# Layer norms of a five-attention decoder: the normalising step moved from VectorE to ScalarE, with a shift made on GpSimd

## What is computed

```python
def _layernorm(x, axis=-1, eps=1e-05):
    m = jnp.mean(x, axis=axis, keepdims=True)
    v = jnp.var(x, axis=axis, keepdims=True)
    return (x - m) / jnp.sqrt(v + eps)
```

## Time and profile before

| | |
|---|---|
| median of 3 runs | 3958.57 us (3949.79 to 3959.46) |
| the profiled execution's own time | 3954.29 us |
| its span, first to last instruction | 3952.6 us |
| TensorE busy, granted clock | 3343.7 us (85%), 0.895 of full |
| VectorE busy | 2807.9 us (71%) |
| ScalarE busy | 2094.5 us (53%) |
| GpSimd busy | 975.9 us (25%) |
| TensorE's wait for the first x | 72.1 us |

### The profile page before, as it was taken

One profiled execution on the slowest core, in us unless ns is written; L12 is line 12 of the kernel. 1 busy time (PEld: TensorE's weight loads), 2 busy tenths in 40 slices (PEclk: granted clock), 3 DMA queues, 4 the chain that ended last, 5 costly groups with the idle time before them and its releaser, 6 DMA issues. The chain is left out here.

```text
span 3952.6 us, 94629 instructions
## 1 busy us (share of the span) xinstructions
PE 3343.7 (85%) x38960; PEld 2374.8 (60%) x38960; DVE 2807.9 (71%) x6362; ACT 2094.5 (53%) x4222; POOL 975.9 (25%) x1808
## 2 busy tenths in 40 slices
PE   1889888989898888888988888899888898988886
PEld 1666565666565656656656656566655665655554
DVE  5777776777776767777776667677776677777664
ACT  4745565455556554564564555645555556455551
POOL 0312341122222321131132222212342112124310
PEclk9989888988898889888988988898988898989887
DMA  5000000000000000000000000000000000000000
GB/s 163 3 3 2 2 3 4 9 7 3 2 2 2 8 3 7 7 3 2 7 2 2 5 4 7 6 4 2 1 2 3 9 9 4 2 2 2 1 4 6
DMA packets 30365, 31.49 MB, mean 8 GB/s; under 512 B 8673, under 2 KB 26482, under 8 KB 29938
## 3 DMA queue, kind: packets, MB, share of 16 engines
q1 hardware_dynamic: 29938, 25.44, 2.1%
HBM read 21.24 MB, written 4.19 MB: 6 GB/s over the span
## 5 line engine op out<-in xcount | busy, mean ns | idle before, releaser
L1103 ACT ACTIVATE p<-bank,p_log 128x512 f32<-128x512 f32 (+2 forms) x1280 | 746.8, 583 | 1331.3 <-PE bank L797 1266.6
L1669 POOL TENSOR_TENSOR prob<-p,prob 120x256 f16<-120x256 f32 (+2 forms) x512 | 455.5, 890 | 1742.4 <-ACT prob L1104 1741.3
L1104 ACT ACTIVATE prob<-bank,p_log 128x512 f16<-128x512 f32 (+2 forms) x1280 | 747.3, 584 | 0.0
L1368 DVE TENSOR_REDUCE negm<-bank 128x2 f16<-128x512 f32 (+1 forms) x1280 | 675.3, 569 | 33.9 <-PE bank L752 18.2
L1286 DVE TENSOR_TENSOR prob<-p,prob 128x512 f16<-128x512 f32 (+2 forms) x768 | 474.0, 624 | 188.9 <-ACT prob L1104 178.8
L774 PE MATMUL bank<-q,k 32*128 32x256 f16 (+2 forms) x6144 | 496.8, 289 | 65.1 <-issue 34.7
L668 PE MATMUL bank<-w_exp,ident_h 128*128 128x512 f16 x1280 | 429.3, 421 | 32.3 <-DVE negm L1368 15.2
L1678 POOL TENSOR_SCALAR_AFFINE_SELECT probm<-prob 128x128 f16<-128x128 f16 x1024 | 325.9, 358 | 340.4 <-DVE prob L1286 340.4
L774 PEld LDWEIGHTS bank<-q,k 32*128 32x128 f16 (+1 forms) x6144 | 307.9, 110 | 142.7 <-issue 66.8
L797 PE MATMUL bank<-ident_h,negm 128*128 128x256 f16 (+2 forms) x2560 | 384.9, 273 | 0.0
L1661 POOL TENSOR_TENSOR rstd<-veps,minus_half 128x2 f32<-128x2 f32 (+1 forms) x208 | 149.7, 720 | 887.9 <-DVE veps L1261 887.3
(11 more groups left out here) (300 smaller groups left out, 6286.5 us busy)
## 6 DMA issues: line engine op xcount, KB each, us to landing
x<-in_x SPq DMA_DIRECT2D x16, 256.0 KB, 2.7
out<-z SPq DMA_DIRECT2D x16, 256.0 KB, 2.2
xa<-in_li SPq DMA_DIRECT2D x9, 256.0 KB, 4.6
x<-in_li SPq DMA_DIRECT2D x7, 256.0 KB, 4.3
z<-in_wq SPq DMA_DIRECT2D x4, 256.0 KB, 4.4
z<-in_li SPq DMA_DIRECT2D x4, 256.0 KB, 4.1
cx<-in_ctx_t SPq DMA_DIRECT2D x16, 60.0 KB, 1.8
cx<-in_ctx SPq DMA_DIRECT2D x16, 60.0 KB, 1.8
```

Source lines behind the costliest of these rows:

```text
L1103: act(p32[0:n, g % PBUF32, 0:cols], ps[0:n, 0:cols], ACT.Exp, bias=p_log[0:n, :], scale=a.scale)
L1104: act(prob[0:n, 0, g % PBUF, 0:cols], ps[0:n, 0:cols], ACT.Exp, bias=p_log[0:n, :], scale=a.scale).then_inc(a_done, one(a_done))
L1368: v.tensor_reduce(negm[:, h * NT:(h + 1) * NT], ring_v[bank_of(e, v_full)][:, :].rearrange("p (t n) -> p t n", t=NT)[:, :, 0:ATTNS[k].keys ...
L1669: g.tensor_tensor(prob[0:n, 1, m % PBUF, 0:cols], p32[0:n, m % PBUF32, 0:cols], prob[0:n, 0, m % PBUF, 0:cols], ALU.subtract).then_inc(pp_ ...
```

## The change

`norm_end` is gone. The normalising step is `norm` on ScalarE: an Identity activation of x times rstd plus a shift, one instruction a tile, where shift is minus mean times rstd. VectorE's `norm_begin` also makes `back`, which is minus the mean. GpSimd's `root` makes the power as before, waits for it by a semaphore of its own (`root_made`), and multiplies `back` by the root into `shift`.

The stages out2, experts3, norm2, norm4, ctx2, h3 and r3 now exist on ScalarE alone (`SCALAR_ONLY`), and the tables place them anew, along with some others: h0, h1 and h2 for k = 4 at turns 20, 21 and 24 where they were at 22, 23 and 26.

For k = 3 the first two norms share one set of sums: the second norm's variance is v / (v + eps), so both roots are one power on four columns (`twice`), and ScalarE writes both results out of x, first the normed norm into xa, then the norm into x. That leaves 12 rounds of sums and roots a sample, 192 in all, and 400 normalising instructions as before (384 of 128x256 and 16 of 120x128). VectorE waits for ScalarE's norm ahead of `gain`, and ahead of a `norm_begin` for the norm before the last, whose buffers it takes.

```diff
 EARLY = {
     0: (),
-    1: (("oT", 9), ("out", 11), ("out2", 12)),
-    2: (("oT", 9), ("out", 11), ("out2", 12), ("xT_e", 15), ("router", 17), ("best", 21), ("experts", 23), ("experts2", 27), ("experts3", 30)),
-    3: (("oT", 9), ("out", 12), ("norm2", 15), ("norm3", 17), ("norm4", 20)),
-    4: (("oT", 9), ("out", 11), ("out2", 12), ("ctx", 16), ("ctx2", 17), ("xoT", 18), ("h0", 22), ("h1", 23), ("h2", 26), ("norm3", 28), ("norm4", 29)),
-    TAIL: (("oT", 9), ("out", 11), ("out2", 12), ("xoT", 16), ("h0", 18), ("h1", 21), ("h2", 25), ("h3", 26), ("xT", 29), ("sel", 31)),
+    1: (("oT", 9), ("out", 11), ("out2", 13)),
+    2: (("oT", 9), ("out", 11), ("out2", 13), ("xT_e", 15), ("router", 17), ("best", 21), ("experts", 23), ("experts2", 27), ("experts3", 29)),
+    3: (("oT", 9), ("out", 12), ("norm2", 14), ("norm3", 16), ("norm4", 19)),
+    4: (("oT", 9), ("out", 11), ("out2", 13), ("ctx", 15), ("ctx2", 17), ("xoT", 18), ("h0", 20), ("h1", 21), ("h2", 24), ("h3", 26), ("norm3", 28), ("norm4", 30)),
+    TAIL: (("oT", 9), ("out", 11), ("out2", 13), ("xoT", 16), ("h0", 18), ("h1", 21), ("h2", 25), ("h3", 27), ("xT", 29), ("sel", 31)),
 }
...
-VECTOR_ONLY = ("out2", "experts3", "norm4", "h3", "r3", "ctx2")
+SCALAR_ONLY = ("out2", "experts3", "norm2", "norm4", "ctx2", "h3", "r3")
...
-        minus_half = sb("minus_half", [P, NT])
+        minus_half = sb("minus_half", [P, 2 * NT])
...
-        veps = [sb(f"veps{i}", [P, NT]) for i in range(2)]
-        rstd = [sb(f"rstd{i}", [P, NT]) for i in range(2)]
+        veps = [sb(f"veps{i}", [P, 2 * NT]) for i in range(2)]
+        rstd = [sb(f"rstd{i}", [P, 2 * NT]) for i in range(2)]
+        back = [sb(f"back{i}", [P, NT]) for i in range(2)]
+        shift = [sb(f"shift{i}", [P, 2 * NT]) for i in range(2)]
...
                         if k == 3:
-                            yield
                             gain_rows(0)
...
+                def norm(src, dst, ready, n=P, nt=NT, again=None):
+
+                    i = norms[0] % 2
+                    norms[0] += 1
+                    e.wait_ge(rstd_ready, norms[0])
+                    for to, c in ((dst, 0),) if again is None else ((again, nt), (dst, 0)):
+                        for t in range(nt):
+                            last = act(to[0:n, t, :], src[0:n, t, :], ACT.Identity, bias=shift[i][0:n, c + t:c + t + 1],
+                                       scale=rstd[i][0:n, c + t:c + t + 1])
+                    last.then_inc(ready, 1)
...
-                        if k == 3:
-                            yield
-                            yield
+                        if k <= 2:
+                            norm(x[lane], x[lane], z_ready[lane])
+                        elif k == 3:
+                            norm(x[lane], x[lane], xn_ready, again=xa[lane])
+                            yield
+                            yield
+                            wait_sent(k, b)
+                            norm(xa[lane], zk, z_ready[lane])
+                        else:
+                            wait_sent(k, b)
+                            norm(xs, zk, zo_ready)
+                        yield
...
+                        norm(x[lane], x[lane], z_ready[lane])
+                        yield
...
+                    if k == 4:
+                        own = cx[lane][:, :].rearrange("p (a f) -> p a f", a=1)
+                        norm(own, own, zc_ready, n=CTX_TOK, nt=1)
+                        yield
...
                         yield from hidden_layer(k, "h", ACT.Gelu, b_li2[i])
                         if k == 4:
-                            yield
+                            norm(xa[lane], xa[lane], xn_ready)
+                            yield
+                            yield
+                            norm(xa[lane], zk, z_ready[lane])
+                        else:
+                            norm(zk, zk, z_ready[lane])
+                        yield
                     if k == 5:
...
+                        norm(zk, zk, out_ready)
+                        sends[z_of(k, b)] += 1
+                        yield
...
-                def norm_begin(src, n=P, nt=NT):
-
-                    i = norms[0] % 2
-                    norms[0] += 1
+                norms = []
+
+                def norm_begin(src, ready, n=P, nt=NT, twice=False):
+
+                    i = len(norms) % 2
+                    if len(norms) >= 2:
+                        e.wait_ge(*norms[-2])
                     for t in range(nt):
                         v.bn_stats(stats[i][0:n, t], src[0:n, t, :]).then_inc(dve_step, one(dve_step))
                     e.wait_ge(dve_step, sent(dve_step))
                     for t in range(nt):
                         v.bn_aggr(mv[i][0:n, t], stats[i][0:n, t]).then_inc(dve_step, one(dve_step))
                     e.wait_ge(dve_step, sent(dve_step))
+                    if twice:
+                        v.tensor_scalar(veps[i][0:n, nt:2 * nt], mv[i][0:n, 0:nt, 1], 1.0 + EPS, EPS * EPS,
+                                        ALU.mult, ALU.add).then_inc(dve_step, one(dve_step))
+                    v.tensor_scalar(back[i][0:n, 0:nt], mv[i][0:n, 0:nt, 0], -1.0, None, ALU.mult
+                                    ).then_inc(dve_step, one(dve_step))
                     v.tensor_scalar(veps[i][0:n, 0:nt], mv[i][0:n, 0:nt, 1], EPS, None, ALU.add
                                     ).then_inc(var_ready, one(var_ready))
-                    return norms[0]
-
-                def norm_end(number, src, dst, ready=dve_step, n=P, nt=NT):
-
-                    i = (number - 1) % 2
-                    e.wait_ge(rstd_ready, number)
-                    for t in range(nt):
-                        signal = dve_step if t < nt - 1 else ready
-                        v.tensor_scalar(dst[0:n, t, :], src[0:n, t, :], mv[i][0:n, t, 0:1], rstd[i][0:n, t:t + 1],
-                                        ALU.subtract, ALU.mult).then_inc(signal, one(signal))
-                    e.wait_ge(dve_step, sent(dve_step))
-                    e.wait_ge(ready, sent(ready))
+                    norms.append((ready, sent(ready) + one(ready)))
 
                 def gain(s):
 
+                    e.wait_ge(*norms[-1])
...
                         if k <= 2:
                             add_bank(x[s], x[s])
-                            number = norm_begin(x[s])
-                            yield
-                            norm_end(number, x[s], x[s], z_ready[s])
+                            norm_begin(x[s], z_ready[s])
                         elif k == 3:
                             add_bank(x[s], x[s])
-                            number = norm_begin(x[s])
+                            norm_begin(x[s], xn_ready, twice=True)
                         else:
-                            wait_sent(k, b)
                             add_bank(xs, xa[s])
-                            number = norm_begin(xs)
-                            yield
-                            norm_end(number, xs, zk, zo_ready)
+                            norm_begin(xs, zo_ready)
                         yield
                         if k == 3:
-                            norm_end(number, x[s], x[s])
-                            number = norm_begin(x[s])
-                            yield
-                            norm_end(number, x[s], xa[s])
                             gain(s)
-                            number = norm_begin(xa[s])
-                            yield
-                            wait_sent(k, b)
-                            norm_end(number, xa[s], zk, z_ready[s])
+                            norm_begin(xa[s], z_ready[s])
...
                         yield from hidden_layer("hidden", k, b, hidT, xa[s])
                         if k == 4:
-                            number = norm_begin(xa[s])
-                            yield
-                            norm_end(number, xa[s], xa[s])
+                            norm_begin(xa[s], xn_ready)
+                            yield
                             gain(s)
-                            number = norm_begin(xa[s])
-                            yield
-                            norm_end(number, xa[s], zk, z_ready[s])
+                            norm_begin(xa[s], z_ready[s])
                             yield
                         else:
                             v.tensor_tensor(flat(zk), flat(x[s]), flat(xa[s]), ALU.add).then_inc(x_free, one(x_free))
                             e.wait_ge(x_free, sent(x_free))
                             freed["x", b] = x_free, sent(x_free)
-                            number = norm_begin(zk)
-                            yield
-                            norm_end(number, zk, zk, z_ready[s])
+                            norm_begin(zk, z_ready[s])
...
-                def root(n=P, nt=NT):
+                def root(n=P, nt=NT, twice=False):
 
                     e.wait_ge(var_ready, upcoming(e, var_ready))
-                    i = sent(rstd_ready) % 2
```

(47 more changed lines are left out.)

## The result

The change made the kernel slower: 4014.46 us median of 4 runs (4008.5 to 4020.89) against 3957.7 us, a ratio of 1.0139, 95% interval 1.0117 to 1.016. The forecast was 3918, 1.0% faster; 4014 lies above its range of 3860 to 3992.

The account below looks back on a forecast made before the run. The prediction took TensorE to be held up by VectorE, 335 us of its waits. 87 us won from VectorE's backlogs against 47 us of losses gave net -40 us, forecast 3918 us, 1.0% faster, range 3860 to 3992.

Parts of the forecast that it names:

- The loads and the indicators: Expected profile: VectorE 2615 us, ScalarE 2360, GpSimd 1000; TensorE's VectorE waits under 220, ScalarE norm waits 110 to 140.
- losses: Time added: direct path 11, table loads 10, GpSimd 5, kernel end 1, ScalarE's own waits 20; together 47 us.
- the store: TensorE waits behind VectorE backlogs containing normalising work: 145 us, of which 60%, 87 us, would be won.
- direct path: From root to norm's end in 68 norms TensorE waits for: longer chain against shorter norm, net +11 us.
- ScalarE's own: TensorE's waits for ScalarE, whose load grows by an eighth and whose norms hold up moves: +20 us (0 to 60).
- GpSimd's: Products queue ahead of the addition of xa and the low exponentials: TensorE waits 5 us more for GpSimd.
- I would be wrong if the product takes 0.7 us: GpSimd's two-column product, taken as 0.2 us; at 0.7 us, 68 places would lose 34 us, eating the gain.
- The turns: Fourth attention's moved h0 and h1 add 16 Gelu loads and 16 back; half of the former count, 10 us.
- the prediction's own signs of being wrong: VectorE's wait sum doesn't fall, product takes 0.7 us, or VectorE's low parts wait for ScalarE until backlogs form again.
- Rival 2: Time saved behind VectorE is spent on longer chains through GpSimd and ScalarE: 48 against 47 us, 3957 us, chance 0.15.
- Rival 3: In ScalarE's in-order queue, norms waiting for their shift stand ahead of exponentials: slower, 3994 us, chance 0.22.
- the excess: VectorE's o_tok norms take 0.849 us beside GpSimd's addition; their extra length leaves by the port rule, but might stay on ScalarE.

Follow-up runs that it names:

- back_behind_veps: Changed kernel with shared sums, k = 1, 2, 4 and z-in-place norms back on VectorE with plain root, back made after veps: 3925.29 us, ratio 0.9895.
- h_moved_only: The kernel before with only the fourth attention's h0, h1, h2 moved to turns 20, 21, 24 from 22, 23, 26: ratio 1.0069.

## Why the prediction was wrong

- **The loads and the indicators** came near the forecast: VectorE 2622 us, GpSimd 1009, the product 0.208 us, 63 Gelu loads, tailT 0.89 us later, VectorE's sum of waits 177, norms on ScalarE 130. ScalarE has 2321 instead of 2360; its norm takes 0.60 us and a pair 1.09 instead of 1.03. Every effect for which the sum had a term was found, and the sum has the wrong sign.
- **The step that failed** is the balance of the sum, losses of 47 us against 87 us out of the store. In TensorE's waits the losses are 95 us (direct path 23, ScalarE's own 53, GpSimd's 18), and the store gave 50. TensorE's busy time, 19 us longer, had no term; its waits for issue fell by 13. Together that is the 54 us of the two spans within 3.
- **The direct path** was +11 and came out at +23. It charged the longer chain (negation, product, semaphores) against a shorter norm. The chain alone, with the norm left on VectorE, puts the same 23 us on these waits, and costs 46 us in all. "I would be wrong if the product takes 0.7 us" was the wrong condition: at 0.2 us the product alone cost the kernel before 31 us.
- **The turns** were counted as half of 16 loads, 10 us. On the kernel before they cost 27, of which 16 come from h2, whose move the prediction didn't price at all.
- **ScalarE's own waits** were +20 (0 to 60), beside the 10 of the loads. Those that aren't norms rose from 95 to 148 us, +53. GpSimd's waits rose by 18 instead of 5. No run splits these sums further.
- **The store** was taken at 60%, 87 us. VectorE's waits without the norms fell from 228 to 177, 50 us: the lower bound, a third. One of the prediction's own signs of being wrong did come: VectorE stands 308 us for ScalarE's exponentials, 179 before. How much of the missing 37 us this took is not shown.
- **Rival 2** came nearest in its terms: it had the store right, at 48 us, and the losses at half of what they were. **Rival 3** named ScalarE's queue and a time of 3994; at the norms of z in place it is worth roughly 15 to 18 us. On the kernel before, the chain (1.16%) and the turns (0.69%) each lose by themselves; they add up to more than the loss of 1.39%. Either they hide each other in part, as turns and standing did, or the rest of the change gains; no run separates the two.

## What to carry to other kernels

Before an operation is moved to an engine with room, price every instruction and semaphore that joins its dependency chain. Here two operations on two columns cost 0.22 to 0.25 us for each norm that had them, in three comparisons, though TensorE waits right behind only a third of the norms. Give the new inputs only to the instances that need them: that won back 0.6 and 0.9 points. The fastest version also makes them beside the long operation and not ahead of it, but its last gain lies in TensorE's busy time and isn't explained. Test the added chain alone, with nothing moved, and compare TensorE's waits and its busy time separately: a version can win in one and lose in the other.

## What the runs showed of the hardware

VectorE's normalising instruction has two lengths. In the view of its line before, from o_tok, where GpSimd adds xa at the same time (min/median/max):

```profile
L1271 DVE TENSOR_SCALAR z<-o_tok,mv,rstd x64: 400/754/1343, 491.3 to 3894.7; 128x256 f32<-128x256 f32 x64
```

With the product ahead of GpSimd's addition the median rises to 1236 ns: the instructions of over 1 us grow from 29 to 35 of 64, and those of under 0.45 us fall from 19 to 9. On ScalarE the same work takes 584 to 634. The Trainium skill ("SBUF — State Buffer", "Who interferes with whom") says that VectorE's two-port operations and GpSimd lock each other out and ScalarE never waits; these three rows agree, and the prediction's doubt whether the excess moves along is answered: it doesn't.

The mean granted clock differs between runs of one kernel: of 19 runs of before on one chip the shortest, 3948.89 us, stood at 0.897 and one of 3969.62 us at 0.888. It differs between kernels too: the 7 runs of before beside back_behind_veps stood at 0.888 to 0.894 and its 4 at 0.901 to 0.905. But it doesn't rank them: h_moved_only lost 27 us at 0.896 to 0.898, where before stood at 0.888 to 0.896 beside it. No run here separates the clock from the waits.
